# Pipelined blocks between two attentions of an adaLN transformer, one core

## The reference

```python
mod = silu(c) @ wmod                       # six vectors of 512 per sample
h = layernorm(x) * (1 + ca) + sa
x = x + ga * attn(h)                       # ga, gb: |.| at least 0.25
h = layernorm(x) * (1 + cb) + sb
x = x + gb * ffn(h)
# layer 0 attn: 32 heads, latent of 32 + rope of 64, values through the latent; causal
# layer 0 ffn: h @ W_base.T + b + sum_e sparsemax(router(h))_e * (h @ A_e) @ B_e   (8 experts, rank 16)
# layer 1 attn: 32 query heads of 16, one key and value head; causal
# layer 1 ffn: h @ W_base.T + b + fixed low-rank update (masked coefficients, inverse Fourier)
```

## Time and profile before

| what | us |
|---|---|
| three runs | 2380.11, 2401.78, 2393.92; median 2393.92 |
| profiled execution, its span | 2393.23, 2391.4 |
| TensorE, VectorE, ScalarE, POOL busy | 2041.1 (85%), 1155.3 (48%), 875.1 (37%), 480.4 (20%) |
| opening | 0 to 137 |
| lead-in of the first attention | 137 to 212 |
| its 16 steps | 212 to 1172 |
| `feed0`, twice | 1172 to 1466 |
| `queries1`, twice | 1466 to 1632 |
| second attention | 1632 to 2237 |
| `feed1`, twice | 2237 to 2391 |

### The profile page before, as it was taken

How to read it: one execution, slowest core, us unless ns; L and a number is a source line. 1 busy time by engine, 2 the same in 40 slices (tenths; PEclk the granted TensorE clock), 3 DMA queues, 4 the chain that set the end, 5 groups by cost and what they waited for, 6 DMA issues and landing times. The chain is left out here.

```text
span 2391.4 us, 34019 instructions
## 1 busy us (share of the span) xinstructions
PE 2041.1 (85%) x12632; PEld 1169.2 (49%) x12632; DVE 1155.3 (48%) x2506; ACT 875.1 (37%) x1825; POOL 480.4 (20%) x375
## 2 busy tenths in 40 slices
PE   6648999999999999999578684856999999999578
PEld 4425666666666666656334242533444444444233
DVE  3426555555555555554023242224666676562245
ACT  3402444444444444444301011220466666566112
POOL 0021444444444444442300000000000000001000
PEclk9767999999999999999889897776799999898789
DMA  8732223222222232221140501134222222211230
GB/s 285 258 106 54 55 72 73 72 72 72 70 69 63 68 75 71 69 67 47 46 171 18 198 13 65 71 113 82 33 43 37 41 47 48 41 23 21 93 119 35
DMA packets 95047, 183.80 MB, mean 77 GB/s; under 512 B 26394, under 2 KB 31162, under 8 KB 94754
## 3 DMA queue, kind: packets, MB, share of 16 engines
q1 hardware_dynamic: 94882, 181.63, 27.9%
HBM read 95.94 MB, written 29.38 MB: 52 GB/s over the span
## 5 line engine op out<-in xcount | busy, mean ns | idle before, releaser
L912 ACT ACTIVATE at_prob<-at_scp 128x512 f32<-128x512 f32 (+1 forms) x608 | 349.3, 575 | 534.9 <-PE at_scp L1013 525.9
L946 DVE CUSTOM_DVE_ANT_0 at_junk<-at_mxp,causal 128x128 f32<-128x128 f32 (+3 forms) x512 | 240.6, 486 | 327.0 <-PE at_mxp L1022 322.8
L1543 ACT ACTIVATE as_prob<-as_scp 128x512 f32<-128x512 f32 (+2 forms) x640 | 309.3, 564 | 212.2 <-PE as_scp L1637 157.6
L1022 PE MATMUL at_mxp<-l_khi,at_qhi 96*128 96x512 f32 (+2 forms) x768 | 263.9, 409 | 6.6 <-DVE at_tm L970 6.4
L1009 PE MATMUL at_scp<-at_qhi,l_khi 97*128 97x512 f32 (+1 forms) x608 | 260.6, 429 | 8.2 <-issue 4.4
L1591 DVE TENSOR_REDUCE as_mxd<-as_mxp 128x2 f32<-128x256 f32 (+3 forms) x256 | 203.7, 821 | 118.1 <-PE as_mxp L1656 115.9
L1576 POOL TENSOR_TENSOR l_att_t<-l_att_t,as_spread 64x1024 f32<-64x1024 f32 x16 | 37.9, 2367 | 1011.9 <-DMA as_spread<-l_recips 1011.9
L1012 PE MATMUL at_scp<-at_qlo,l_khi 96*128 96x512 f32 (+1 forms) x608 | 234.9, 386 | 0.0
L1013 PE MATMUL at_scp<-at_qhi,l_klo 96*128 96x512 f32 (+1 forms) x608 | 233.9, 385 | 0.0
L1634 PE MATMUL as_scp<-as_q,l_keys 49*128 49x512 f32 (+2 forms) x640 | 215.8, 464 | 14.4 <-ACT as_prob L1543 11.9
L1651 PE MATMUL as_mxp<-l_keys,as_q 48*128 48x512 f32 (+2 forms) x768 | 189.1, 471 | 39.9 <-DMA as_q<-scratch_queries 17.1
(11 more groups left out here) (204 smaller groups left out, 2737.5 us busy)
## 6 DMA issues: line engine op xcount, KB each, us to landing
at_qhi<-at_shi SPq DMA_DIRECT2D x192, 128.0 KB, 2.4
at_qlo<-at_slo SPq DMA_DIRECT2D x192, 128.0 KB, 2.4
op_ring<-in_wmod SPq DMA_DIRECT2D x12, 1024.0 KB, 7.2
op_ring<-in_wo_t SPq DMA_DIRECT2D x8, 1024.0 KB, 12.2
at_spread<-l_recips SPq DMA_DIRECT2D x64, 128.0 KB, 2.7
l_o<-at_u_sb SPq DMA_DIRECT2D x16, 512.0 KB, 3.2
as_q<-scratch_queries SPq DMA_DIRECT2D x48, 128.0 KB, 4.7
as_q<-l_queries_b SPq DMA_DIRECT2D x48, 128.0 KB, 4.3
```

The source lines that it names most:

```text
L912: nc.scalar.activation(prob[:, x % RING0, c0:HALF], scp[x % BANKS0][:, c0:HALF], ACT.Exp).then_inc(s["exp_done"], 1)
L946: nc.vector.tensor_tensor_reduce(out=junk[:, u % 2, 0:w], in0=tile[:, 0:w], in1=k.causal[:, HALF - w:HALF], scale=1.0, scalar=LOWEST, op0= ...
L1022: nc.tensor.matmul(bank("max", t, u)[:, 0:w], qhi[t % 2][0:KR, j, qt * P:(qt + 1) * P], k.khi[0:KR, t // NG, k0:k0 + w], start=True, stop= ...
L1543: nc.scalar.activation(prob[:, x % RING1, cols], scp[x % BANKS1][:, cols], ACT.Exp).then_inc(s["exp_done"], 1)
```

## The change

- **Opening.** `xt` has four slots, x(2) and x(3) wait for nothing and are issued earlier; `vo` has eight slots and one store of 2 MB at the end; stores of gates and of the joined update matrix come last; the coefficients' loads come before the rope tables.
- **Lead-in.** Maxima of step 0 begin after its own projections; step 1's six projections lie after maximum 12 and after maximum 30.
- **First attention.** The maxima of the next step begin at place 1, not 2.
- **Middle.** `prime`, `clear`, `feed0` and `queries1` are replaced by one block over 23 slots (`middle`). Tiles of both samples follow each other; each piece of a tile's work has its own slot. The attention output comes tile by tile (256 KB) into six buffers, x stays in SBUF for the second norm, semaphores of the attention are cleared on POOL inside this block.
- **Closing.** The weights and gates are loaded in the second attention, after its third step's moves are issued. `closing` is one block over 16 tiles.

```diff
-MAX_AT = {2: 5, 3: 5, 4: 5, 5: 8, 6: 5, 7: 8, 8: 5, 9: 7}
+MAX_AT = {1: 4, 2: 4, 3: 6, 4: 5, 5: 8, 6: 5, 7: 8, 8: 4, 9: 4}
...
+def lead_in():
+    pieces = [("queries", 0, u) for u in range(PJ)]
+    for u in range(UNITS):
+        pieces.append(("max", 0, u))
+        if u + 1 in (UNITS // 4, 5 * UNITS // 8):
+            pieces += [("queries", 1, i) for i in (range(3) if u < UNITS // 2 else range(3, PJ))]
+    return pieces
...
                 def joined_out(g):
                     act.wait_ge(s["vo_psum"], g + 1)
-                    if g >= 2:
-                        act.wait_ge(vo_out[g % 2], 16 * (g // 2))
-                    nc.scalar.activation(vo[:, g % 2, :], bank("vo", g)[:], ACT.Copy).then_inc(s["vo_done"], 1)
+                    nc.scalar.activation(vo[:, g, :], bank("vo", g)[:], ACT.Copy).then_inc(s["vo_done"], 1)
...
                     for i in range(TH):
                         if i + 1 < TH:
                             modulated(first + i + 1)
-                        if i == 0 and g + 1 < GH:
-                            deviation(g + 1)
                         if i == TH - 1:
+                            if g + 1 < GH:
+                                deviation(g + 1)
                             squares(first)
@@ middle, TensorE
+                for slot in range(SLOTS_M):
+                    if slot < ALL:
+                        project(slot)
+                    if 0 <= slot - 1 < ALL:
+                        turn_first(slot - 1)
+                    for kind, g, m in shared_uses(slot):
+                        if kind == "lt":
+                            turn_low(g)
+                    if 0 <= slot - FEED < ALL:
+                        feed(slot - FEED)
+                    if 0 <= slot - 1 < ALL:
+                        low_products(slot - 1)
+                    if 0 <= slot - TURN2 < ALL:
+                        turn_second(slot - TURN2)
+                    for kind, g, m in shared_uses(slot):
+                        if kind == "kv":
+                            keys_values(g)
+                        if kind == "q":
+                            queries(g, m)
+                        if kind == "kt":
+                            turn_keys(g)
@@ middle, ScalarE
+                for slot in range(SLOTS_M):
+                    if slot < ALL:
+                        deviation(0, slot, "meanvar_done", "std_done")
+                    if 0 <= slot - 1 < ALL:
+                        modulate_first(slot - 1)
+                    for kind, g, m in shared_uses(slot):
+                        if kind == "lt":
+                            low_out(g)
+                    if 0 <= slot - FEED < ALL:
+                        deviation(1, slot - FEED, "meanvar2_done", "std2_done")
+                    if 0 <= slot - TURN2 < ALL:
+                        modulate_second(slot - TURN2)
+                    for kind, g, m in shared_uses(slot):
+                        if kind == "q":
+                            query_hi(g, m)
@@ middle, VectorE
+                for slot in range(SLOTS_M):
+                    if slot < ALL:
+                        first(slot)
+                    if 0 <= slot - FEED < ALL:
+                        second(slot - FEED)
+                    if slot % TH == 0 and 0 < slot <= ALL:
+                        experts(slot // TH - 1)
@@ closing, TensorE
+                for slot in range(LAST):
+                    if slot < ALL:
+                        project(slot)
+                    if 0 <= slot - 2 < ALL:
+                        turn(slot - 2)
+                    if 0 <= slot - FEED1 < ALL:
+                        feed(slot - FEED1)
```

More of the change, by code:

```diff
@@ L144, in _ @@
                     sp.sem_clear(sem)
-def prime(nc, sems):
-    with nc.Block() as block:
-        @block.sync
-        def _(sp):
-            for name, sem in sems.items():
-                if "_in" not in name:
-                    sp.sem_inc(sem, CREDIT)
 WSLOTS = 5
@@ L719, in quad_work @@
     return pieces
+def lead_in():
[5 more added lines that the diff above has]
+    return pieces
 def bank_order():
-    order = [("queries", t, u) for t in range(2) for u in range(PJ)] + [("max", 0, u) for u in range(UNITS)] + [("turn", 0, 0)]
+    order = lead_in() + [("turn", 0, 0)]
     for t in range(STEPS0):
@@ L1439, with shared_uses @@
         "mt_ready mrow_done u_moved sum_out sum_in recip_done recip_out recip_in att_done")
+ALL = B * TILES
+GH = B * HALVES
+OSLOTS, XSLOTS, HSLOTS = 6, 6, 6
+FEED, TURN2, QUERY = 5, 6, 10
+SLOTS_M = ALL + TURN2 + 1
+def shared_uses(s):
+    uses = []
+    for g in range(GH):
+        if s == TH * g + FEED:
+            uses.append(("lt", g, 0))
+    for g in range(GH):
+        pieces = [[("kv", g, 0), ("q", g, 0)], [("kt", g, 0), ("q", g, 1)], [("q", g, 2)], [("q", g, 3)]]
+        first = TH * g + QUERY
+        for i, group in enumerate(pieces):
+            if s == min(first + i, SLOTS_M - 1):
+                uses += group
+    return uses
@@ L1570, in _ @@
             def _(pool):
+                for sem in stale.values():
+                    pool.sem_clear(sem)
                 def normalise(t):
@@ L1787 @@
+                for slot in range(LAST + 1):
+                    if slot < ALL:
+                        first(slot)
+                    if 0 <= slot - FEED1 - 1 < ALL:
+                        second(slot - FEED1 - 1)
+                    if slot < ALL:
+                        normalise(slot)
 class Kept:
@@ L1890, in build @@
+        closing(nc, k, scratch["x_mid"], out, closed)
+        clear(nc, closed)
+def build(nc, t, out, scratch):
     nc.disable_value_cache = True
```

956 lines of the change are left out of this document (471 added, 485 removed).

## The result

The changed kernel takes 2287.9 us (median of 4 runs, 2283.6 to 2291.6) against 2391.9 before: a ratio of 0.957, 95% interval 0.952 to 0.961. It is faster by 104 us where 167 were forecast, outside the range of 2198 to 2262. The profiled execution has a span of 2289.8.

The account below looks back on a forecast made before the run. TensorE was taken to bound the long stretches, with savings in its idle time between blocks and waits inside them. The terms -13 - 10 + 10 - 10 - 111 - 3.5 - 29 = -166.5 gave 2227 us, range 2198 to 2262.

Parts of the forecast that it names:

- the first attention's +10: First attention, 16 steps: +10 us (-15 to +27), from waits for moves +11, covered exponentials -4, joins +3.
- The 4 that the maxima in place 1 were to cover: First attention: four maxima between scores cover some of the waits for ScalarE's exponentials, -4 us.
- The size of the wait, 0.8 us: First attention, place 1: the first maximum waits 0.8 us for the last high move in 14 steps, +11 us.
- the attention loses more: Rival: join held in all 15 steps for 2.6 us and query wait at 1.9: +35, 2262 us; chance 0.07.
- The opening: Opening: ScalarE's waits for stores go, so TensorE's wait of 12.93 us goes: -13 us (0 to -16).
- The lead-in: Before the first score: step 0's maxima begin earlier, first score at 202.7 against 212.55: -10 us (-8 to -11).
- the gap: Between first attention and first projection: clearing blocks go, fewer bytes are waited for: -10 us (-6 to -14).
- the exit: Middle to second attention: two blocks of clearing go from 17.06 us idle: -3.5 us (-2 to -5).
- the gap before closing and closing: Closing: early weight loads -5.2, two batches in one block -23.8, together -29 us (-22 to -31).
- The middle: Middle: one block of 23 slots takes 315 us in place of 426.1: -111 us (-90 to -115).
- The rival in which the low products wait in every slot: Rival, middle: VectorE late to the first residual, slots 5 to 15 keep the 4 us: +44, 2271 us; chance 0.12.
- The joins: First attention: joins of maxima shift about 0.9 us against POOL; 12 of 15 waits kept, counted as +3 us.

Follow-up runs that it names:

- r7_wait: Changed kernel with maxima from place 2 as before, plus a TensorE wait in place 1 for the next step's high-part moves: 2278.3 us, ratio 0.956.
- r3_dev: Changed kernel with the opening's square root back beside the first tile of a half, as before the change: 2268.1 us, ratio 0.952.
- r8_lead: Changed kernel with the old table of maxima and the lead-in as before the change: 2216.4 us, ratio 0.930.
- r9_late: Changed kernel with the old table of maxima and the closing stage's loads issued at its start: 2217.5 us, ratio 0.932.
- r2_swap: Changed kernel with ScalarE in the middle modulating tile s-1 before the square root of tile s: 2264.4 us, ratio 0.946.
- r10_join1: Changed kernel with one-input join, maxima from place 1 with a semaphore per head, middle's and opening's square roots moved: 2186.8 us, ratio 0.918.
- r11_join2: Changed kernel with one-input join, old table of maxima, middle's and opening's square roots moved: 2178.8 us, ratio 0.915.
- r12_old: Kernel before the change with only the join of maxima made a one-input reduction: 2376.7 us, ratio 0.9946.
- r4_one: Changed kernel with one maximum in place 1, behind its third score, in place of four: 2258.8 us, ratio 0.944.

## Why the prediction was wrong

The step that failed is the third, the first attention's +10. It measured +67.3: 38.6 of waits for the moves, 22.7 of longer busy time, 1.8 more of waits for joins (15.6 against 13.8 in the steps), and 4 of small gaps. The 4 that the maxima in place 1 were to cover of ScalarE's exponentials did not show: TensorE's idle time ahead of scores was 5.4 before and 6.5 after. Two things in it were wrong.

*The size of the wait, 0.8 us, was read from the wrong step.* The forecast placed the end of the score before the first maximum at 461.4, with the moves issued from 452.87: 8.5 us between them. That is step 4, whose join was held. Behind that wait the values ahead of place 0 ran at the lower clock. TensorE, kernel before, the turn of the maxima and the values of step 4, and those of step 10, whose join was short, with that step's idle time ahead of place 0 and its last matmul ahead of where the first maximum would be, and SyncE's issues:

```profile
450.94 0.28 PE L1028 MATMUL at_mxp<-ident,at_mxd 128*32 128x128 f32 x1 [1.70 <-DVE at_mxd L951]
...
452.12 3.21 PE L1041 MATMUL at_op<-at_prob,l_cn 128*32 128x512 f32 x16
```

```profile
818.73 0.28 PE L1028 MATMUL at_mxp<-ident,at_mxd 128*32 128x128 f32 x1
...
819.99 1.71 PE L1041 MATMUL at_op<-at_prob,l_cn 128*32 128x512 f32 x16
...
824.08 0.47 PE L1009 MATMUL at_scp<-at_qhi,l_khi 97*128 97x512 f32 x1 [0.88 <-issue]
...
828.63 0.33 PE L1013 MATMUL at_scp<-at_qhi,l_klo 96*128 96x384 f32 x1
```

```profile
822.54 7.52 SPq L788 DMA_DIRECT2D at_qhi<-at_shi  x12
```

3.21 us against 1.71 for the same sixteen records: 1.5 us of cover that a step without that fall of the clock does not have; it fell in five of the eight steps with a held join. In step 10 the maximum would have come at 828.8, 6.3 behind the first issue and not 8.5. The other 0.7 comes from the hold itself. It keeps TensorE's turn back until 2.96 us behind the join's start, against 1.09 in step 10, but not the moves: in 13 of the 15 steps these do not wait for the last scores but for ScalarE's copies behind POOL's last operation, and are issued 4.9 behind the join's start in both. Of these 1.9 us step 10 makes up most, since it idles for 1.1 us later on, ahead of its scores. With 7.52 of issues and the 1.8 to the landing that the changed kernel shows, the last move is there at 831.9: 3.1 us of waiting, the size that was measured (2.6 on average, 3.20 in the step shown). Of 15 such places one was read, and it was the one with the shortest wait of all. The same two times, the landing of the last move and the start of the place's next score, read in all 15 steps of the trace of the kernel before, give 0.8 to 4.5 us and 38.4 in sum; 38.6 were measured. So this part of the miss stood in that trace.

The changed kernel has both kinds. TensorE in one of its steps with a held join, turn and first maximum:

```profile
453.88 0.28 PE L938 MATMUL at_mxp<-ident,at_mxd 128*32 128x128 f32 x1 [1.96 <-DVE at_mxd L861]
...
465.26 0.39 PE L932 MATMUL at_mxp<-l_khi,at_qhi 96*128 96x256 f32 x1 [0.77 <-DMA at_qhi<-at_shi]
```

0.77 us, the forecast's 0.8. In its eight steps with a held join the waits are 0.68 to 3.55, 1.9 on average: 0.68 to 1.77 in the four where the granted clock fell behind the join, 2.38 to 3.55 in the four where it did not. In six with a free one they are 3.11 to 4.69, 3.5 on average.

*The clock behind the wait was left out.* The forecast charged a wait by its length. r7_wait shows that 48.7 us of waits cost 25 more in slower matmuls, since TensorE falls from 2.4 to 1.2 GHz behind them (3.2 us each on average). The row that could have told it was shown: 0.76 for a matmul that takes 0.50 elsewhere, and the text even allowed "1 for colder matmuls" in the lead-in. The forecast's rival "the attention loses more" named the right place, with 1.9 for the wait and joins held on top, 35 in all; it too had no clock in it, and was given 0.07.

*The opening (-13, measured -8.2).* ScalarE's waits for stores went as forecast. The change also moved a square root, which the forecast did not price at all; VectorE, in order, waits for it and hands ScalarE its raw products late. r3_dev gives 4.7 of it back.

*The lead-in (-10, -9.9), the gap (-10, -10.1), the exit (-3.5, -4.1), the gap before closing and closing (-29, -28.2)* came out by the working; r8_lead and r9_late confirm the lead-in and the part of the early loads. In the lead-in 36.8 us were measured from the landing of the moves to the first score, and 36.4 forecast (its 7.6 for the projections on VectorE is 7.9 by its own factors). The tail is 1.5 longer.

*The middle (-111, -103.5).* Its mechanism was right: the wait in slots 1 to 4 was 3.74 to 3.83 (forecast 4.05), slots from 5 on have none, and the experts' wait in slot 17 was 3.15 (3.4), seen in the rows below. What was short is the price of the four waits, 13.7 a slot in place of 12.4, for the slower matmuls behind them (r2_swap), and slot 0's 10.6 in place of 8.8. From slot 5 on the forecast's sum was 256.8, and 257.0 were measured; that hit is partly luck, since its own prices for that work (290.5 less what lies in slots 0 to 4, and the wait of 3.4) come to 253.7. The rival in which the low products wait in every slot (2271) lies nearest to the measured time, but its mechanism did not occur: from slot 5 on they waited for nothing.

```profile
1503.31 1.12 PE L1213 MATMUL ml_shared<-ident,ml_low 128*128 128x128 f32 x4 [3.15 <-DVE ml_low L1405]
...
1557.47 10.57 PE L1244 MATMUL ml_shared<-ml_h_t,ml_wq 128*128 128x512 f32 x24 [0.98 <-DVE ml_q_lo L1417]
1581.02 0.58 PE L1659 MATMUL as_mxp<-l_keys,as_q 48*128 48x256 f32 x2 [12.97 <-DMA as_q<-scratch_queries]
```

From 1245.30 to 1567.9 it is 322.6. TensorE waits 12.97 for the second attention's first queries. The closing stage answers to the earlier trace rows:

```profile
2162.70 13.50 PE L1757 MATMUL fg_yps<-l_wo,l_att_t 128*128 128x512 f32 x24 [17.06 <-PEq L65]
...
2276.16 7.03 PE L1773 MATMUL fg_fps<-l_wf,fg_h_t 128*128 128x512 f32 x16
```

From 2162.70 to 2283.0 it is 120.3, forecast 120; one projection, one turn and one product follow each other without a gap from the fourth tile on.

*The joins.* The forecast kept their waits nearly as they were (+3), and +1.8 was measured, which is luck. That the join only moves by 0.9 us against POOL did not keep them the same: they were held 8 times for 3.4 us, not for 2.9, and the other kernels with the two-input join had 1 to 11 held of 16. A held join and POOL beside it, in the changed kernel, with the join's line:

```profile
450.41 3.41 DVE L861 TENSOR_TENSOR at_mxd<-at_mxd,at_mxf 128x16 f32<-128x16 f32 x1
```

```profile
448.93 2.40 POOL L769 TENSOR_TENSOR at_u_sb<-at_u_sb,at_spread 128x1024 f32<-128x1024 f32 x1
...
452.51 1.28 POOL L748 TENSOR_TENSOR at_tm<-at_tm 128x512 f32<-128x512 f32 x1
```

```profile
L861 DVE TENSOR_TENSOR at_mxd<-at_mxd,at_mxf x16: 174/2310/3424, 191.3 to 1166.2; 128x16 f32<-128x16 f32 x16
...
  PE at_mxp L938: 17.2, 9
```

and a free one in the kernel before:

```profile
387.90 0.42 DVE L951 TENSOR_TENSOR at_mxd<-at_mxd,at_mxf 128x16 f32<-128x16 f32 x1
```

```profile
385.91 2.37 POOL L859 TENSOR_TENSOR at_u_sb<-at_u_sb,at_spread 128x1024 f32<-128x1024 f32 x1
```

The free one starts 1.99 us into POOL's long operation and ends when that one ends, at 388.28 to 388.32. The one of the earlier trace rows starts 1.97 into it and ends two operations later; so does the one above, 1.48 into it. The Trainium skill ("SBUF — State Buffer", "Who interferes with whom" and the summary behind it) says that a VectorE operation with two inputs in SBUF contends with a GpSimd operation that reads SBUF, that a reduction, with its single input, does not, and that the loser is blocked until the other's instruction is over. The runs agree with the first two: 0.185 to 0.188 us in all joins of r10_join1, r11_join2 and r12_old. By the third no join would be held beyond the end of the one operation that it meets; here joins were held through two more, 3.41 in place of 0.9. What decides between the two was not found. It is not the start alone: in the kernel before, joins that start 1.97 us into the operation came out free (at 634.07 and 817.64) and held (at 447.98), and one that starts 1.99 into it was held:

```profile
756.74 2.90 DVE L951 TENSOR_TENSOR at_mxd<-at_mxd,at_mxf 128x16 f32<-128x16 f32 x1
```

*The second attention* was 6.5 us shorter, where nothing was changed in its work. r12_old, which doesn't touch it, has 565 too, so this is within what its code does from one execution to the next (558 to 571 in all the profiles).

## What to carry to other kernels

Price a new wait on TensorE by its length and by what stands behind it: here each of 15 waits of 3.2 us on average cost another 1.7 us in slower matmuls. In r4_one waits of up to 1.1 us cost their own length alone; there and in the kernel before, waits of 1.5 to 2.0 lowered the clock in some steps and not in others. When a term is one place times fifteen steps, read that place in several steps and ask which of them runs undisturbed: a held operation upstream had hidden most of this wait, and all fifteen steps of the same trace, read one by one, give the sum to within 1 us. And an early start needs early data: a wait for the last of twelve transfers undid it, a semaphore for each head took the wait away, and even then the early start was worth nothing.

## What the runs showed of the hardware that was not expected

- A 128x16 operation of VectorE with two SBUF inputs took 0.17 to 0.18 us with POOL idle, 0.41 to 1.24 when it was let in at the end of the POOL operation it met, and 2.5 to 3.4 when it was not and stayed out until POOL stopped. Joins with the same start to 0.01 us went either way. As a reduction with one input it took 0.19 in all 48 cases of three kernels.
- Fifteen waits in the first attention, 3.2 us on average and one in each 68 us, lowered the mean granted clock of the stage from 1.00 to 0.96 (r7_wait). Waits of 1.70 to 1.73 for a held join were followed by a stretch at half clock in five of eight steps of the kernel before.
